# A block of attention and eight experts: the passage between its two halves spread over later groups, and two projections of modulation vectors placed later

## What is computed

```
mod = silu(c) @ wmod                      # per batch: sa, ca, ga, sb, cb, gb
ga, gb = sign * max(|.|, 0.25)
h = layernorm(x) * (1 + ca) + sa
x = x + ga * attention(h)                 # causal, rope on q and k
h = layernorm(x) * (1 + cb) + sb
gate = softmax(h @ Wg + bg); thr = sigmoid(h @ Wt + bt) * 0.125
w = max(gate - thr, 0), normalised over the experts
x = x + gb * sum_e w[e] * (gelu(h @ W1[e] + b1[e]) @ W2[e] + b2[e])
```

## Time and profile before

| | |
|---|---|
| time, median of 3 runs | 1741.76 us (1741.69 to 1743.46) |
| the profiled execution's own time | 1742.58 us |
| its span | 1740.7 us, 26364 instructions |
| PE busy | 1721.9 us (99%), 8408 matmuls |
| PEld, DVE, ACT, POOL busy | 1447.7, 1215.3, 990.9, 998.7 us |
| chain that ended last | PE 84%, each other engine at most 1% |
| mean granted TensorE clock | 0.998 |
| transfers | 72.54 MB, mean 42 GB/s |

### The profile page before, as it was taken

One profiled execution on the slowest core, in us unless ns is written; L12 is line 12 of the kernel. 1 busy time (PEld: TensorE's weight loads), 2 busy tenths in 40 slices (PEclk: granted clock), 3 DMA queues, 4 the chain that ended last, 5 costly groups with the idle time before them and its releaser, 6 DMA issues.

```text
span 1740.7 us, 26364 instructions
## 1 busy us (share of the span) xinstructions
PE 1721.9 (99%) x8408; PEld 1447.7 (83%) x8408; DVE 1215.3 (70%) x2275; ACT 990.9 (57%) x1794; POOL 998.7 (57%) x1649
## 2 busy tenths in 40 slices
PE   8999999999999999999999999999999999999998
PEld 7889888997888888888888888888888888888887
DVE  6777778767776666666666678766666666666676
ACT  4766666655655555555555556555555555555553
POOL 5644556336264755647484849374847566574843
PEclk9999999999999999999999999999999999999999
DMA  4100000012112112111211121122301011121202
GB/s 114 29 22 19 26 25 25 11 34 57 25 37 50 49 25 49 37 37 37 37 49 28 46 34 40 61 64 83 110 22 52 25 49 37 37 37 37 37 12 61
DMA packets 92058, 72.54 MB, mean 42 GB/s; under 512 B 11024, under 2 KB 90128, under 8 KB 91920
## 3 DMA queue, kind: packets, MB, share of 16 engines
q1 hardware_dynamic: 91776, 70.79, 15.6%
q10 hardware_dynamic: 144, 0.07, 0.0%
HBM read 62.32 MB, written 8.52 MB: 41 GB/s over the span
## 4 chain that ended last, share of the span: by engine, by line
PE 84%; DVE 1%; issue 1%; ACT 1%; DMA 1%; POOL 0%; SPq 0%; DVEq 0%; ACTq 0%; POOLq 0%
PE bank L1079 13%; PE bank L1077 13%; PE bank L1078 13%; PE bank L1038 11%; PE bank L1040 11%; PE bank L1039 11%; PE bank L962 2%; PE bank L988 1%; PE bank L1002 1%; PE bank L950 1%; PE bank L951 1%; PE bank L949 1%; PE bank L884 1%; PE bank L874 1%; PE bank L983 1%
## 5 line engine op out<-in xcount | busy, mean ns | idle before, releaser
L1342 ACT ACTIVATE g_sb<-c_sb,b_cols 128x512 f32<-128x512 f32 x384 | 276.2, 719 | 399.9 <-DVE c_sb L1787 292.7
L1663 DVE TENSOR_TENSOR h_lo<-g_sb,h_hi 128x512 fp32r<-128x512 f32 x512 | 390.6, 783 | 101.5 <-ACT h_hi L1346 101.2
L1077 PE MATMUL bank<-h_hi,w_both 128*128 128x512 f32 x1024 | 398.9, 390 | 1.1 <-DVE h_lo L1663 1.1
L1079 PE MATMUL bank<-h_lo,w_both 128*128 128x512 f32 x1024 | 398.7, 389 | 0.0
L1078 PE MATMUL bank<-h_hi,w_both 128*128 128x512 f32 x1024 | 398.4, 389 | 0.0
L1944 POOL TENSOR_TENSOR h2f<-h2f,y_sb 128x256 f32<-128x256 f32 x216 | 201.4, 965 | 286.5 <-DVE y_sb L1687 286.5
L1038 PE MATMUL bank<-t_hi,w_hi 128*128 128x512 f32 x896 | 351.8, 393 | 4.6 <-ACT p_u L1374 2.9
L1040 PE MATMUL bank<-t_hi,w_lo 128*128 128x512 f32 x896 | 348.9, 389 | 0.0
L1039 PE MATMUL bank<-t_lo,w_hi 128*128 128x512 f32 x896 | 348.8, 389 | 0.0
L1346 ACT ACTIVATE h_hi<-c_sb,b_cols 128x512 fp32r<-128x512 f32 x384 | 272.2, 709 | 0.0
L1077 PEld LDWEIGHTS bank<-h_hi,w_both 128*128 128x128 f32 x1024 | 192.2, 188 | 41.5 <-DVE h_lo L1663 1.5
(11 more groups left out here) (184 smaller groups left out, 2901.9 us busy)
## 6 DMA issues: line engine op xcount, KB each, us to landing
w_raw<-w_dram SPq DMA_DIRECT2D x128, 256.0 KB, 3.0
g_rows<-gates_scratch SPq DMA_DIRECT2D x32, 512.0 KB, 8.6
x_sb<-x_dram SPq DMA_DIRECT2D x32, 128.0 KB, 2.2
x_scratch<-x_sb SPq DMA_DIRECT2D x32, 128.0 KB, 1.7
x_slabs<-x_scratch SPq DMA_DIRECT2D x4, 512.0 KB, 7.8
out_dram<-x_slabs SPq DMA_DIRECT2D x4, 512.0 KB, 3.2
h2f<-x_scratch SPq DMA_DIRECT2D x4, 512.0 KB, 3.7
wmod_raw<-wmod_dram SPq DMA_DIRECT2D x4, 256.0 KB, 3.8
```

Source lines behind the costliest of these rows:

```text
L1077: nc.tensor.matmul(o, w_hi, h_hi[:, ring, :], start=first, stop=False, skip_group_check=True)
L1079: done_ = nc.tensor.matmul(o, w_hi, h_lo[:, ring, :], start=False, stop=last, skip_group_check=True)
L1342: nc.scalar.activation(g_sb[:, m % 2, :], source, ACT.Gelu_apprx_tanh, bias=bias).then_inc(act_g, 1)
L1663: nc.vector.tensor_tensor(h_lo[:, m % RING, :], g_sb[:, m % 2, :], h_hi[:, m % RING, :].bitcast(F32), ALU.subtract).then_inc(dve_lo, 1)
```

## The change

PRE_AFTER moves the second batch's rows from behind the `qkv` of tile 3 to tile 6, and its gates from tile 4 to tile 7; nearly every number of PATIENCE is another. In the expert half, of tile 31 only `Y`, the residual and the statistics stay in group 0, the statistics behind the group's low parts; the root goes to group 4, the transposes to 5, the router to 6, the exponentials to 8, the gates' transposes to 12. POOL splits slice 2 ahead of anything of tile 31, and SP loads slices 2 and 3 ahead of tile 31's x1. Gelu's table is loaded by an instruction of its own ahead of group 0. Block c12 of group 0 gets its gelu in group 1, behind ACT's copy of bank_a. The sums of the second tokens go to the ends of groups 1 and 2, their low parts to group 3. The gates of batch 1 are stored ahead of slice 12, not 9.

```
-PRE_AFTER = (None, 0, 2, 3, 4)
+PRE_AFTER = (None, 0, 2, 6, 7)
-    "PE": {"aT": 452, "bT": 777, "qkv": 886, "rotT": 552, "Y": 651, "pre": 1131, "gate": 1051, "S": 717,
-            "T": 815, "PV": 830},
+    "PE": {"aT": 317, "bT": 763, "qkv": 900, "rotT": 652, "Y": 728, "pre": 521, "gate": 1147, "S": 699,
+            "T": 785, "PV": 845},
...
-        GATES0_AT, LATE_TURN_AT, LATE_GATE_AT, LATE_EXP_AT, GATES1_AT = 0, 1, 2, 5, 11
-        GATES_STORED = 9
+        GATES0_AT, LATE_ROOT_AT, LATE_TURN_AT, LATE_GATE_AT, LATE_EXP_AT, GATES1_AT = 0, 4, 5, 6, 8, 12
+        GATES_STORED = 12
+        SECOND_LOW = (T2, T3, T1, T4)
...
+                    if i == TILES - 1:
+                        for q in (2, 3):
+                            sp.wait_ge(pool_split, (q - 1) * SPLIT_STEPS)
+                            load_weights(sp, q)
...
-                for q in range(2, B * E * FS):
-                    if q == 3:
-                        store_gates(0)
-                        load_gates(0)
+                store_gates(0)
+                load_gates(0)
+                for q in range(4, B * E * FS):
...
+                act.preload_act_table_set("gelu_apprx_tanh_and_others")
                 for n in range(GROUPS):
...
-                    if n == 0:
+                    if n == 1:
+                        hidden(0, "c12", c_sb[:, 0, :])
+                    if n == LATE_ROOT_AT:
                         root(TILES - 1 + BEHIND)
...
+                def second_sums(*names):
+                    x, t = h2f[:, 0, 1, :, :], lambda part: t_f32[1][:, part - T1, :]
+                    b11, b12, b21, b22 = (x[:, k, u * UTOK:(u + 1) * UTOK] for k in range(KD) for u in range(2))
+                    for part in names:
+                        i = SUMS.index(part)
+                        if i in (1, 2):
+                            dve.wait_ge(dve_tsum, i)
+                        plus, minus = ((b12, b11), (b22, t(T1)), (b21, t(T2)), (b22, b12))[i]
+                        nc.vector.tensor_tensor(t(part), plus, minus, ALU.subtract).then_inc(dve_tsum, 1)
+                def second_low(*names):
+                    dve.wait_ge(dve_tsum, 3)
+                    for part in names:
+                        dve.wait_ge(act_tsum, SECOND_LOW.index(part) + 1)
+                        nc.vector.tensor_tensor(t_lo[1][:, part, :], t_f32[1][:, part - T1, :],
+                                                t_hi[1][:, part, :].bitcast(F32), ALU.subtract).then_inc(dve_tlo, 1)
...
                     if n == 0:
-                        dve.wait_ge(*done(dve_x1, "Y", TILES - 1))
+                        statistics(TILES - 1 + BEHIND)
+                    if n == 1:
+                        second_sums(T1, T2)
+                    if n == 2:
+                        second_sums(T4, T3)
+                    if n == 3:
+                        second_low(T1, T4)
+                    if n == LATE_ROOT_AT:
                         normalise_x1(TILES - 1)
...
+                        if n == 1:
+                            low(0, "c12")
                         if n > 0:
                             low(n, "c11")
...
+                split(2)
                 add_eps(TILES - 1 + BEHIND)
-                inverse_root(TILES - 1 + BEHIND)
-                split(2)
                 split(3)
                 tokens(0, 1)
+                inverse_root(TILES - 1 + BEHIND)
```

More of the change, by code:

```diff
@@ L258 @@
 PATIENCE = {
-    "PE": {"aT": 452, "bT": 777, "qkv": 886, "rotT": 552, "Y": 651, "pre": 1131, "gate": 1051, "S": 717,
-            "T": 815, "PV": 830},
-    "ACT": {"aT": -4842, "bT": 465, "qkv": 67, "rotT": -475, "O": -752, "norm": 252, "pre": -4492, "wq": -3,
[4 rows of a table removed]
-    "POOL": {"xa": 311, "rope": -1774, "norm": -583, "rstd": -3599, "traw": 2780, "split": -6008},
+    "PE": {"aT": 317, "bT": 763, "qkv": 900, "rotT": 652, "Y": 728, "pre": 521, "gate": 1147, "S": 699,
+            "T": 785, "PV": 845},
+    "ACT": {"aT": -2875, "bT": -6042, "qkv": -91, "rotT": -6896, "O": -1868, "norm": -42, "pre": -4070,
[4 rows of a table added]
+    "POOL": {"xa": 898, "rope": 257, "norm": -1133, "rstd": -696, "traw": 6996, "split": -7038},
 }
@@ L1052, in tokens_ready @@
                             pe.wait_ge(*done(dve_low, "tlo", (T1, T2, T4, T3).index(b_)))
+                    elif b == 0:
+                        if b_ in (B11, B21, B22):
+                            pe.wait_ge(pool_tlo, (B11, B21, B22).index(b_) + 1)
+                        else:
+                            pe.wait_ge(dve_tlo, (T2, T3, T1, T4).index(b_) + 1)
                     else:
@@ L1360, in cast_tokens @@
                             "p (u n) -> p u n", u=2), ACT.Copy).then_inc(act_traw, 1)
[L1361 to L1367, removed]
+                    elif b == 0 and f > 1:
+                        for part in ((T2,), (T3, T1, T4))[f - 2]:
+                            act.wait_ge(dve_tsum, SUMS.index(part) + 1)
+                            nc.scalar.activation(t_hi[p][:, part, :], t_f32[p][:, part - T1, :],
+                                                 ACT.Copy).then_inc(act_tsum, 1)
+                    elif b > 0 and f < FS - 1:
+                        for i, part in enumerate((T1, T3) if f == 1 else (T2, T4)):
+                            act.wait_ge(dve_tsum, k * 4 + 2 * f + i - 1)
+                            nc.scalar.activation(t_hi[p][:, part, :], t_f32[p][:, part - T1, :],
+                                                 ACT.Copy).then_inc(act_tsum, 1)
+                act.preload_act_table_set("gelu_apprx_tanh_and_others")
                 for n in range(GROUPS):
@@ L1388, in _ @@
                     act.wait_ge(dve_c12, n + 1)
-                    hidden(n, "c12", c_sb[:, 0, :])
+                    if n > 0:
+                        hidden(n, "c12", c_sb[:, 0, :])
             @block.vector
@@ L1761, in _ @@
                     ends = n % FS == 0 and n > 0
-                    if 0 < n <= GROUPS:
+                    if 1 < n <= GROUPS:
                         low(n - 1, "c12")
@@ L1765, in _ @@
                         residual(TILES - 1, m_banks[1])
-                        statistics(TILES - 1 + BEHIND)
                     if ups:
@@ L1774, in _ @@
                         evict(n - 2, 1)
-                    if n % FS != 1 and n >= FS - 1:
+                    if n % FS != 1 and n >= FS:
                         sum_tokens(n)
+                    if n == FS - 1:
+                        second_low(T2)
                     if ups:
@@ L1795, in _ @@
                         between(n)
+                    if n == 0:
+                        low(n, "c11")
+                    if n == FS - 1:
+                        second_low(T3)
                     if n % FS == 1 and n >= FS:
@@ L1801, in _ @@
                         nc.vector.tensor_tensor(c_sb[:, 0, :], bank_h, u2[:], ALU.add).then_inc(dve_c12, 1)
-                    if n == 0:
-                        low(n, "c11")
                     if ups:
@@ L1807, in _ @@
                         finish_late(n)
-                    if n < FS - 1:
-                        sum_tokens(n)
                 turn(GROUPS)
```

## The result

| | before | after |
|---|---|---|
| median, runs on one chip | 1742.67 us (1741.69 to 1744.09, 15 runs) | 1745.72 us (1743.0 to 1748.19, 15 runs) |
| ratio | | 1.0019, 95% interval [1.0012, 1.0026] |
| profiled execution, own time | 1742.58 us | 1744.96 us |
| span | 1740.7 us | 1743.2 us |
| first matmul of the experts | 405.25 us | 408.28 us |

The change is 3 us slower where 3.9 us of gain were forecast. The last two rows split it, for the profiled executions: attention ends 3.03 us later, and the experts give back only 0.5 us.

The account below looks back on a forecast made before the run. PE was taken to bound the kernel, busy 1721.9 of 1740.7 us. Passage 4.0 - 0.4 + 0.1 - 0.2 + 0.4 = 3.9 us, attention 0: 1742.58 - 3.9 = 1738.7, median 1737.9; forecast's own range 1735.5 to 1740.5, for all 1733 to 1743.5.

Parts of the forecast that it names:

- the term of attention: Attention, up to 405 us: new orders taken to gain 0, with 1.5 us to each side.
- my rival for the second stretch at the low clock: Attention right behind 34 us: a gap reopens, 2.5 us idle and 3.5 us of half clock, giving 1743.9; chance 8%.
- the new orders of attention give it back: Attention: short waits of 0.2 to 0.4 us at some ten places cost 2 to 4 us, median 1741; chance 15%.
- the rows win nothing by their place: Attention from 34.03 us: moving batch 1's rows, 2.79 us of PE, saves no PE work; other work is slowed instead.
- my rival on the early clock: Before 31.2 us: new order fills the gap, clock stays 2.4 GHz, 3.5 + 1 us gained, median 1733.4; chance 18%.
- groups 0 and 1: Start of the experts: group 2 starts 4.2 us earlier, 4.0 net of the transposes, range 3.0 to 4.8.
- two more loads of 1.28 us: Root in group 4: exp and ln table, then gelu's again; the pair is covered with 0.4 us to spare, costs 0.
- My charge for groups 4 and 8: A 1.4 us eviction stands in the same group as the pair of table loads: 0.2 us for both, 0 to 0.8.
- the sums of the tokens: Ends of groups 1 and 2, while POOL is splitting: sums take up to 1.24 us; PE charged 0.4 us, 0 to 1.2.
- the rival in which the passage only moves its waits: Groups 1 to 3: DVE and POOL hinder each other, c22 and u3 late; gain 1, median 1740.8; chance 7%.
- slice 2 and the gates of batch 1: Slice 2 loaded before attention ends; gates stored ahead of slice 12 end DVE's wait until 540.10 us, giving 0.4 us.
- The signs I had named as wrong: PE idle above 1 us from 36 to 405, changed half-clock stretch count, or waits for p_u and c_sb in groups 2-9.

Follow-up runs that it names:

- attn_new: Kernel before with the new PRE_AFTER and PATIENCE alone, nothing of the expert part: 1747.3 us, ratio 1.0028.
- few_fills: Kernel after without 14 of the 58 idle matmuls that TensorE issues in early gaps: 1745.08 us, ratio 1.0022.
- passage_new: Kernel after with the old placing and old patience, so the new expert part alone: 1740.55 us, ratio 0.9989 to the kernel before.
- root_two: Kernel after with the table holding both ln and exp loaded by name ahead of the root in group 4: 1743.41 us, ratio 1.0009.
- bt_last: Kernel after with the transposes of tile 30 moved behind the last PV of tile 31 on TensorE: 1744.39 us, ratio 1.0011.
- sums_spread: Kernel after with VectorE's four sums of the first tokens set singly instead of three in a row: 1745.36 us, ratio 1.0024.
- passage_root: New expert part with old placing and patience, and the ln and exp table loaded by name: 1738.43 us, ratio 0.9982 to the kernel before.
- tokens_late: New expert part, old attention, root's table by name, GpSimd's low parts of the second tokens held back behind group 2's last product: 1739.8 us, ratio 0.9989.
- passage_root_b: Second run of the new expert part with old attention and the root's table loaded by name: 1739.13 us, ratio 0.9979 to the kernel before.

## Why the prediction was wrong, point by point

**Step that failed: "Between these far ends I take 0", the term of attention.** It measured +3.0 us in the profile of after and +3.7 in that of attn_new (+4.7 by its median). I argued that from 31.2 us on TensorE "is never idle for long" and that the new readers come only with tile 14. Both hold, and neither bears on the question. The 0.29 us of idle time was not slack in the operands, as my rival for the second stretch at the low clock read it; it was the fit of one table of patience to one placing. The square of runs shows it: either half alone costs 30 to 36 us (for the placing, because its rows then come at 179.54 us and not near 59), one tile's difference in the place of the gates costs 6 us, and the pair that belongs together comes out 3 to 4 us behind the old pair. The dense stretch bounded the gain (nothing to win), but I let it bound the loss by the same 1.5 us. The plan that both kernels carry had the answer, 406.5 against 410.0 us, and I did not ask it. My rival "the new orders of attention give it back", 2 to 4 us, was the right case; I had given it 15%, and combined it with a full gain from the passage.

Of the 3 us, 2.05 are idle time in the trace (2.34 against 0.29). After is 1.1 us ahead at 44 us, so some 4 us are lost behind that, about half of it as drawn idle time. attn_new is 0.6 us ahead there and 3.7 behind at the end, which gives the same 4.3: the loss is not the scatter of one start. The rest hides under the drawn ends of matmuls or lies in the order of kinds; the runs don't tell these apart, and it stays open. Why the new pair is the worse of the two fitted pairs stays open too: six edits at its waits found no single place.

**Right: the rows win nothing by their place.** They now stand at 58.40 us and take 1.88 us at full clock instead of 2.79, and other work is slowed in their place. The half-clock stretch shrank to 3.4 us, but what was won by 44 us was lost again by 50. That win isn't the new orders' either: attn_new, with the same orders, has 6.8 us at half clock from 25.39, and the six profiles with the old orders differ by 2.1 us among themselves at 36 us. Nor was the early stretch worth the 3.5 us that my rival on the early clock gave it: few_fills had none and won nothing by 36 us.

**Right in mechanism, too small: groups 0 and 1.** Forecast 4.2 us, 3.0 to 4.8. Without a half-clock stretch it is 22.02 - 16.95 = 5.07 us: the low part of c11 and the copy of bank_a, for which I had left up to 0.3 and 0.1 to 0.6 us of waiting, came in time, in passage_new at these two places (VectorE's timeline, then ScalarE's):

```profile
411.74 0.68 DVE L1679 TENSOR_TENSOR h_lo<-g_sb,h_hi 128x512 fp32r<-128x512 f32 x1
```

```profile
413.77 0.57 ACT L1387 ACTIVATE p_u<-bank 128x512 f32<-128x512 f32 x1
```

In the profile of after a half-clock stretch takes 1.54 of it back. Of the eight kernels profiled with this passage and the new orders, two have it in groups 0 and 1 (after from 408.74 us, root_two from 408.32) and two in the last 8 us of attention (bt_last and sums_spread); the five with this passage and the old orders have none at either place. My rival had such a stretch behind 34 us, not here.

**Wrong: "two more loads of 1.28 us", and so the pair "costs 0".** There were three, and group 4 took 11.35 us instead of 10.20. root_two measured 1.3 us in the first groups, 1.5 to the span's end. My charge for groups 4 and 8 was 0.2, at most 0.8. With two loads group 4 costs nothing, as the step said, but group 8 does: TensorE loses 0.38 us at 501.08 and 0.24 at 506.10 behind its pair of loads at 494.71, together 0.6. An eviction stands in the same group, as the step feared, and no run takes the two apart. The trace of before had shown the form that is free: exponentials alone, one kind of function. The root has two.

**The Trainium skill on tables.** "ScalarE: Activation LUTs", section "Table sets: the hidden batching unit", says that ln followed by exp needs one load, as one set holds both. Here it does so only when that set is loaded by name; left to itself each function brought its own set (450.52 and 452.04 us). The Trainium skill's 2.66 us for a switch (the same page, section "What ACT_TABLE_LOAD costs") are not seen here either: from the load at 450.52 to the start of the function behind it are 1.29 us. With the DRAIN of 1.38 us that it adds to a load, root_two would by my estimate have gained about 2.7 us; it gained 1.3 to 1.5.

**Too small: the sums of the tokens.** Charged 0.4 us, range 0 to 1.2; the wait at 433.85 makes group 2 last 11.48 us. Before it took 11.99, of which 1.8 were the router (group 6, which has the router now, takes 11.99 against 10.20), so 10.2. Group 3 now takes 10.20 instead of 10.49, and the net loss is 1.0. I had the mechanism ("There POOL is splitting too") with 1.24 us for a length; beside GpSimd's token parts it is 1.78. So much of the rival in which the passage only moves its waits came true, in one group and not in three.

**Right: slice 2 and the gates of batch 1.** Slice 2 was loaded at 402.02 us, two later than I named, and hidden. VectorE's eviction at 541.87 waits for nothing, though SP issues its transfer of g_rows only at 513.91 us; side by side the traces differ by 0.6 us there, where I had put 0.4. Group 8 takes that back.

**The sum.** For the passage with two loads I had 3.9 us; passage_root has 1335.45 - 1331.73 = 3.7 us behind the first expert matmul, and passage_new, with the third load, 1335.45 - 1333.28 = 2.2. The prediction's total failed by attention (3.0), the third load (1.5) and the half-clock stretch (1.5); with the 0.2 that the passage is short, these make up the 6.3 us between 1738.7 and 1744.96. That the passage came out at 3.7 for 3.9 is in part luck: groups 0 and 1 gave 0.9 more than forecast, and the token sums and group 8 took as much back.

**The signs I had named as wrong** all came: more than 1 us of idle time between 36 and 405 us, one more half-clock stretch, waits for p_u and c_sb in groups 2 and 4.

## What to carry to other kernels

A stretch without idle time, made by an order that was fitted, has nothing to win but much to lose: price a new order by the idle time that a neighbouring order has, not by what the old one leaves. If the kernel carries the plan that makes its orders, ask it for its planned end before you ask a chip: here it was within 4 us over a range of 32 and put the two fitted pairs 3.5 us apart, though it had the two worst orders the wrong way round. Single waits, on the other hand, are no places to mend such an order: six such edits gained nothing. Count table loads by function, not by visit, and load the set that holds them all by name.

## What the runs showed of the hardware

- **VectorE beside GpSimd.** VectorE's instructions of 128x512 with two inputs from SBUF take 0.68 us alone and 0.87 to 1.79 us beside GpSimd, the least where GpSimd works for a part of the time (421.53 us in after); one that reads a PSUM bank takes 0.68 us in the same stretch (428.56 us, GpSimd busy from 426.34 to 431.02). The Trainium skill, "GPSIMD Engine Reference", section "8. Key points", says that the two engines share their SBUF interfaces, with contention where VectorE has two SBUF inputs; the trace agrees.
- **Half-clock stretches come and go.** At the start of the kernel and where the experts begin, the profiles show 3.4 or 6.8 us at 1.2 GHz, or none; one such stretch in group 0 cost 1.5 us. In the four profiles with this passage that have one between 400 and 412 us, the router's 16 short matmuls end within 1 us ahead of it. But few_fills has the same orders there and no stretch, so this isn't enough to bring one, and the cause stays open.
- **The same attention, up to 2.1 us apart.** The six profiles with the old orders have the first expert matmul between 403.95 us (tokens_late) and 406.07 (passage_root_b). The difference is whole at 36 us and changes by some 0.1 us from there to the experts. tokens_late has 3.4 us at half clock from 24.33 us, passage_root_b 6.8 from 30.21. So attention behind 36 us repeats closely, and a difference of 1 or 2 us between two single first expert matmuls can be the first 36 us alone.
